# Moving the second half's row maxima behind the normalised output on VectorE

## What is computed

```python
x = x + attention(layernorm(x), ctx, ctx)      # 16 heads, softmax over 128 keys
t = rmsnorm(layernorm(x)) * norm_scale
vals, idx = top_k(t @ gate_w.T + gate_b, 4)    # 4 of 32 experts for each token
w = softmax(vals)
out = sum over the 4 experts of w * (swiglu(t @ w1[e].T + b1[e]) @ w2[e].T + b2[e])
x = x + out
```

## Time and profile before

| | |
|---|---|
| timed runs | 240.09, 240.87, 241.19 us; median 240.87 us |
| the profiled execution | 241.15 us, of which the trace's span is 239.3 us |
| busy share of the span | TensorE 71%, VectorE 70%, GpSimd 53%, ScalarE 39% |
| mean granted clock of TensorE | 0.898 of full speed |
| attention stage, steps 0 to 9 | about 24 to 116 us from the span's start |

### The profile page before, as it was taken

How to read it: one execution, slowest core, us unless ns; L and a number is a source line. 1 busy time by engine, 2 the same in 40 slices (tenths; PEclk the granted TensorE clock), 3 DMA queues, 4 the chain that set the end, 5 groups by cost and what they waited for, 6 DMA issues and landing times.

```text
span 239.3 us, 5352 instructions
## 1 busy us (share of the span) xinstructions
PE 169.7 (71%) x1556; PEld 116.9 (49%) x1557; DVE 166.9 (70%) x556; ACT 93.2 (39%) x222; POOL 127.7 (53%) x143
## 2 busy tenths in 40 slices
PE   8306978889888898765596999898999999500000
PEld 3104545546465465442234687677877788400000
DVE  7996586798897999864833867676667676340690
ACT  2001336536465364441202565544555555400210
POOL 9973000136437365375730177777777777777140
PEclk9955799999999999999679999999999999965555
DMA  4229997011528010010114334334333341111851
GB/s 117 87 83 272 257 281 275 3 33 37 176 73 254 27 40 25 24 48 23 34 45 100 75 96 110 109 93 118 103 108 102 92 119 56 45 56 44 244 151 44
DMA packets 28702, 24.39 MB, mean 102 GB/s; under 512 B 4615, under 2 KB 24971, under 8 KB 28683
## 3 DMA queue, kind: packets, MB, share of 16 engines
q1 hardware_dynamic: 25182, 17.68, 27.3%
q0 software_dynamic: 3072, 6.36, 7.7%
q10 hardware_dynamic: 432, 0.15, 0.3%
HBM read 14.53 MB, written 9.12 MB: 99 GB/s over the span
## 4 chain that ended last, share of the span: by engine, by line
PE 34%; DVE 32%; issue 13%; POOL 8%; DMA 5%; ACT 3%; SPq 2%; DVEq 1%; POOLq 0%
PE scores L864 9%; DVE mx L955 7%; PE scores L882 5%; POOL returned L548 4%; DVE sb_part L909 4%; PE scores L862 3%; PE bank L693 3%; PE bank L666 3%; POOL routed L514 2%; DMA fin<-returned 2%; DVE y_all L395 2%; DVE parts L951 2%; PE bank L872 2%; PE bank L833 1%; DVE gs L1144 1%
## 5 line engine op out<-in xcount | busy, mean ns | idle before, releaser
L548 POOL DMA_INDIRECT returned<-y_sb,dest x64 | 63.3, 990 | 34.1 <-ACT y_sb L579 17.1
L514 POOL DMA_INDIRECT routed<-rows,pos x32 | 32.9, 1028 | 29.8 <-DVE pos L1059 23.3
L864 PE MATMUL scores<-w_sb,xtT 128*128 x128 | 38.1, 393 | 0.0
L666 PE MATMUL bank<-ones_bf 128*128 128x512 bf16 x113 | 35.5, 444 | 1.3 <-DVE ones_bf L911 1.0
L1144 DVE TENSOR_TENSOR gs<-glu,sg 128x256 f32<-128x256 f32 x32 | 13.7, 427 | 17.8 <-ACT sg L646 17.5
L882 PE MATMUL scores<-w_sb,hidT 128*128 x128 | 24.8, 302 | 0.0
L579 ACT ACTIVATE hidT<-bank 128x256 f32<-128x256 f32 x32 | 12.3, 384 | 23.9 <-PE bank L872 20.5
L864 PEld LDWEIGHTS scores<-w_sb,xtT 128*128 128x128 f32 x128 | 19.2, 190 | 4.4
L862 PE MATMUL scores<-bias_rows,three_bf 128*128 x64 | 17.6, 275 | 5.2 <-DVE lin L1141 3.3
L955 DVE TENSOR_REDUCE mx<-scores 128x8 f32<-128x1024 f32 x16 | 19.4, 1220 | 1.7 <-PE scores L704 1.7
L882 PEld LDWEIGHTS scores<-w_sb,hidT 128*128 128x128 f32 x128 | 19.3, 191 | 0.8
(11 more groups left out here) (171 smaller groups left out, 354.8 us busy)
## 6 DMA issues: line engine op xcount, KB each, us to landing
xt<-routed SPq DMA_DIRECT2D x64, 66.0 KB
w_sb<-in_w1T SPq DMA_DIRECT2D x8, 512.0 KB
routed<-zeros SPq DMA_DIRECT2D x1, 2112.0 KB, 11.2
w_sb<-in_w2T SPq DMA_DIRECT2D x8, 256.0 KB
fin<-returned SPq DMA_DIRECT2D x8, 256.0 KB, 4.9
returned<-y_sb,dest POOLq DMA_INDIRECT x64
x_sb<-in_x SPq DMA_DIRECT2D x2, 256.0 KB, 5.2
routed<-rows,pos POOLq DMA_INDIRECT x32
```

The lines of the kernel that those rows point to most:

```text
L514: pool.indirect_dma_start(out=routed, out_offset=bass.IndirectOffsetOnAxis(ap=pos[:, par, k:k + 1], axis=0), in_=rows[:, par, k, :], in_of ...
L548: pool.indirect_dma_start(out=returned, out_offset=bass.IndirectOffsetOnAxis(ap=dest[:, buf, h:h + 1], axis=0), in_=y_sb[:, buf, h, :], in ...
L666: pe.matmul(bank[7], ones_bf[:, :], ones_bf[:, None, :].to_broadcast([P, 4, P]), start=True, stop=True)
L864: ins = pe.matmul(dst, xtT[:, par, h, :], w1_sb[:, bass.ds(e, 1), :], start=False, stop=True)
```

## The change

In part a the call `row_max(1)` with its wait for `s_mm[1]` is moved from its place behind `place` to the end of VectorE's step, behind `on`. Nothing is added or left out.

```diff
                 if c:
                     dve.wait_ge(rank_mm, t - 1)
                     dve.tensor_tensor(place[:, :], rank_ps, cst[:, C_BASE:C_BASE + E], ALU.add).then_inc(place_done, 1)
-                if a:
-                    dve.wait_ge(s_mm[1], t + 1)
-                    row_max(1)
                 if c:
                     dve.wait_ge(place_done, t - 1)
                     dve.tensor_tensor(pl_hot[:, :, :], hot[:, :, :], place[:, None, :].to_broadcast([P, K, E]),
                                       ALU.mult).then_inc(plhot_done, 1)
                 if b:
                     o16 = bank[4].rearrange("p (h d) -> p h d", h=H)
                     dve.wait_ge(o_mm, t)
                     dve.reciprocal(rden[:, :, :], o16[:, :, DK:DK + 1]).then_inc(rden_done, 1)
                 if c:
                     dve.wait_ge(plhot_done, t - 1)
                     with nc.allow_low_precision(reason="row numbers below 2**15 are exact"):
                         dve.tensor_reduce(pos[:, par, :], pl_hot[:, :, :], AX.X, ALU.add).then_inc(pos_done, 1)
                 if b:
                     dve.wait_ge(rden_done, t)
                     dve.tensor_tensor(on[:, :].rearrange("p (h d) -> p h d", h=H), o16[:, :, 0:DK],
                                       rden[:, :, :].to_broadcast([P, H, DK]), ALU.mult).then_inc(on_done, 1)
+                if a:
+                    dve.wait_ge(s_mm[1], t + 1)
+                    row_max(1)
```

## The result

| | median | runs |
|---|---|---|
| before | 241.03 us | 240.09 to 241.87, 4 runs |
| after | 246.51 us | 245.96 to 248.16, 4 runs |

The ratio is 1.024, with a 95% interval of 1.018 to 1.030. The median is 5.5 us above that of before. The profiled execution took 245.96 us, 4.8 us more than the profiled one of before, at a mean granted clock of 0.888 against 0.898; the four runs after had 0.888, 0.883, 0.876 and 0.889, and the one at 0.876 is the slowest.

The account below looks back on a forecast made before the run. No engine bounds it everywhere; in the attention loop VectorE is busy 8.95 of 10.10 us. Six steps at 4.40 us less 0.07 for step 7 make +4.3 us, 245.2 us against the 240.87 median; range 243.5 to 247.1.

Parts of the forecast that it names:

- the bounds of the mechanism alone: Whole kernel: the steps' cost taken at its lowest and highest, 3.3 to 5.5 us, giving 244.2 to 246.4 us.
- One of its own signs of being wrong: Attention loop: the prediction called itself wrong if the granted clock is below 1.00 in any step.
- The old place gives nothing back: VectorE ahead of `rden`, steps 1 to 6: it waits 1.1 us for TensorE's transposes instead; gain nothing.
- The new place costs 1.25 us at L965, less the wait of `x2`: VectorE behind `on`: L965 comes 1.25 us later, `x2` 0.69 or 0.82 us later; six steps sum to 4.40 us.
- Step 7 gives 0.07 us: Last moved maxima: `rden` comes 0.30 us earlier, but the logits wait for the gate's product; -0.07 us, within -0.30 to +0.12.
- The clock stays at 1.00 in the loop; chance of the other 0.02, 252 us or more: Attention loop: full clock expected; rival, chance 0.02: it falls, up to 6.7 us per step, 252 us or more.
- The clock at the entrance, 0.06: Rival at the experts' entrance, chance 0.06: the lower clock reaches 3 us into the expert stage, at most 1.5 us; 246.7 us.
- the stretch of the plan: Behind the attention stage, where TensorE runs fillers: lower clock, 0.72 on average over 120 to 124 us, moved by 4.3 us.

Follow-up runs that it names:

- before_short_b: The kernel before with the second half's maxima over 8 of 128 keys from step 1 on, at the old place; 241.27 us, ratio 0.997.
- moved_fill_loop_b: The changed kernel with five fillers instead of two on TensorE behind the output product in steps 1 to 6; 246.62 us, ratio 1.018.
- moved_third: The changed kernel, with no further edit, timed a third time; 248.03 us against 241.76 for the kernel before, ratio 1.022.
- both short kernels of the second set: Kernel before and changed kernel, each with second maxima over 8 of 128 keys from step 1 on; 241.27 and 241.45 us, ratios 0.997 and 0.998.
- moved_again: The changed kernel, with no further edit, once more on a slower chip; 276.31 us against 273.11 for the kernel before, ratio 1.013.
- moved_fill_both: The changed kernel with five fillers instead of two behind the output product and 20 instead of 14 at the experts' entrance; 246.35 us, ratio 1.018.

## Why the prediction came out as it did

The direction and the mechanism were right and the range, 243.5 to 247.1 us, held the 246.51; the likeliest value, 245.2, was 1.3 us low. That the range held it is in part luck: the bounds of the mechanism alone ended at 246.4, and by the profiled execution what came on top was no error of the steps but a lower clock, which the forecast gave a chance of 0.08 in all. One of its own signs of being wrong came true, a clock below 1.00 in a step. By its steps:

- *The old place gives nothing back.* Right: TensorE's 1.94 us from the rank products to the transposes, and before_short_b with a loop of the same length.
- *The new place costs 1.25 us at L965, less the wait of `x2`.* Right, and a little over-sized: the undisturbed six steps cost 0.67, 0.64, 0.66, 0.68, 0.77 and 0.78 us (moved_fill_loop_b less before), 4.20 in place of 4.40. L965 came the forecast 1.25 us later, 1.44 behind the start of `on` where it was 0.19. Two small errors behind it partly cancel. L979 did not get back 0.05 us in each step: into steps 2 and 3 it follows L965 after 0.86 us as before (52.44 to 53.30), later after 0.82 to 0.84. And `x2` follows L979 after 0.07 us (53.30 to 53.37), not the 0.12 that I had estimated; no extra time for its address registers shows in the trace.
- *Step 7 gives 0.07 us.* It gave 0.10 to 0.12. `pos` came 0.28 us sooner behind `m_bf` (2.83 us, 101.67 to 104.50, for 3.11), and the logits came to wait for the gate's product in place of `rows`, as said.
- *The clock stays at 1.00 in the loop; chance of the other 0.02, 252 us or more.* This step failed. The clock was at the lower level for some 3 us in the profiled execution, and from `m_bf` of step 2 to that of 3 and 4 it took 11.10 and 11.14 us where undisturbed it takes 10.72 and 10.71: 0.8 us. moved_third had two such stretches behind step 2, and lost 1.9 us by them from step 3 to step 6 (its steps against those of moved_fill_loop_b). I had priced whole steps at the lower level, up to 6.7 us each, and found them unlikely. What came was a part of a step, and both profiles of the changed kernel on such chips have it. My evidence, a stretch with 2.70 of 4.00 us busy at 1.00, was one execution of another stage and did not bear on it.
- *The clock at the entrance, 0.06.* A loss of the size named came, but by another way, so that the size fits is luck. I had the stretch of the plan reach 3 us into the expert stage. In the profile after, it ended in time, at about 124.5 us (0.73 over 124 to 125 us, 1.00 from there to 131). A new one began between 131 and 132 us, after TensorE had stood idle for 2.29 us ahead of the first tokens, 1.40 before. From the first transpose of the tokens to the third products it took 4.38 us (130.89 to 135.27), before 3.12 (126.65 to 129.77), +1.26 us. moved_third, moved_fill_loop_b and both short kernels of the second set have it too, so the change does not make it alone. Of the 14 profiles, the five with 0.35 to 1.40 us of idle time at this place have 1.00 behind it; of the nine with 1.79 to 2.42 eight have the lower level, and moved_again, with 2.42, has not. The kernel before has one profile, so how often it has the stretch is not known.

The profiled execution adds up: the reciprocal of step 1 comes 0.58 us sooner for reasons ahead of the change, +4.20 and -0.10 for the steps, +0.8 for the clock in the loop, -0.1 between `m_bf` of step 8 and the tokens, +1.26 at the entrance, and from there to the end 0.70 less, which stays unexplained; in sum 4.8 us, as measured. The two clock terms are shown in this trace. That the new gap brings the one in the loop is argued from few profiles: with the three fillers two of two have a loop at 1.00, without them none of two. What share either has in the medians is open, since the fillers in the loop were timed on another chip and filling the entrance moved no median.

## What to carry to other kernels

Before you move an instruction, ask what ends the wait at its old place and who waits at its new one: on an engine that is 89% busy a microsecond can still be free where it stands in front of a later input, and cost its full length two places on. To use a hole, move into it what nobody waits for, and look for semaphore waits between the instructions that are to close up. If an edit adds idle time to TensorE, look at the granted clock in many executions, not in one, and try fillers in the new gap before you judge the edit.

## What the runs showed of the hardware

- The granted clock in a stretch differs between executions of one kernel. With 0.81 to 0.85 us of idle time ahead of L732 in each step of 10.7 us, the profile of after had one stretch at the lower level in the loop (56 us), and that of moved_third two (66 and 80 us) and one ahead of the change's first effect (35 us). Over six executions of moved_third the mean went from 0.870 to 0.896, and the time with it from 249.46 to 245.32 us. With fillers in the gap it stayed within 0.893 and 0.898 in moved_fill_loop_b, but went from 0.884 to 0.901 in moved_fill_both, so the fillers alone do not settle it.
- A stretch at the lower level was 3 to 4 us long in the loop and at the experts' entrance, and cost 0.8 us in the loop of after and 1.26 us at its entrance.
- One chip of the three on which the sets ran took 273 us for the kernel that takes 241 on the others. The four profiles taken there have pauses of up to 1.3 us ahead of ScalarE's second exponential in most steps. What ends them is not in the core's record; the cause was not looked for.
